# Keys and queries kept in memory with the head dimension first, keys padded to 384 columns: a two-layer cross-attention kernel on one Trainium2 core

## The reference

```python
q = hidden_state @ Wq + bq
k = encoder_hidden_state @ Wk + bk
v = encoder_hidden_state @ Wv + bv
q = q.reshape(b, l, KVH, GROUPS, HD).transpose(0, 2, 3, 1, 4)
k = k.reshape(b, s, KVH, HD).transpose(0, 2, 1, 3)
scores = jnp.einsum('bkgld,bksd->bkgls', q, k) * scale
scores = scores + encoder_attention_mask[:, :, None, :, :]
attn = jax.nn.softmax(scores, axis=-1)
out = jnp.einsum('bkgls,bksd->bkgld', attn, v)
x = out @ Wo + bo + hidden_state     # then a layer norm
```

## Time and profile before

| | us |
|---|---|
| median of 3 runs | 677.18 (675.15 to 677.86) |
| profiled execution, device time | 673.3 |
| its span, first to last instruction | 671.5 |
| PE busy | 646.0 (96%) |
| DVE busy | 497.7 (74%) |
| ACT busy, POOL busy | 394.8, 398.4 (59% each) |
| packets of the transfer queue, share of 16 engines | 66.9% |

### The profile page before, as it was taken

One profiled execution on the slowest core, in us unless ns is written; L12 is line 12 of the kernel. 1 busy time (PEld: TensorE's weight loads), 2 busy tenths in 40 slices (PEclk: granted clock), 3 DMA queues, 4 the chain that ended last, 5 costly groups with the idle time before them and its releaser, 6 DMA issues.

```text
span 671.5 us, 11880 instructions
## 1 busy us (share of the span) xinstructions
PE 646.0 (96%) x3737; PEld 470.4 (70%) x3737; DVE 497.7 (74%) x1455; ACT 394.8 (59%) x588; POOL 398.4 (59%) x255
## 2 busy tenths in 40 slices
PE   5998999999999999999999999999999999989987
PEld 2455666777777878777777768787777777756455
DVE  1547787887687787878787878878787888786742
ACT  3232675766657666656766676766567656656421
POOL 4328676775475766667665657676676667554220
PEclk9999898999999999999999999999999999999999
DMA  8898767576785776868584778666786857644212
GB/s 265 266 176 182 182 148 157 124 143 163 141 271 100 244 138 198 162 193 177 130 235 108 230 107 256 123 208 154 198 171 162 193 126 158 116 87 137 89 46 72
DMA packets 61072, 109.67 MB, mean 163 GB/s; under 512 B 11621, under 2 KB 49573, under 8 KB 60498
## 3 DMA queue, kind: packets, MB, share of 16 engines
q1 hardware_dynamic: 61010, 108.91, 66.9%
HBM read 86.37 MB, written 22.10 MB: 162 GB/s over the span
## 4 chain that ended last, share of the span: by engine, by line
PE 71%; DMA 9%; POOL 6%; issue 5%; DVE 3%; SPq 3%; ACT 1%; POOLq 0%; DVEq 0%; ACTq 0%
PE mx_ps L581 11%; PE work L540 10%; PE work L541 9%; PE work L542 9%; PE o_ps L597 7%; PE work L654 5%; PE work L705 5%; POOL pr L2490 4%; DMA late<-r_dr 4%; PE sc_ps L568 3%; PE sc_ps L569 3%; PE sc_ps L561 3%; PE work L610 2%; DMA k_dr<-k_l 1%; PE work L728 1%
## 5 line engine op out<-in xcount | busy, mean ns | idle before, releaser
L1549 DVE CUSTOM_DVE_ANT_0 mx_ps<-mx_ps,mask_n 100x361 f32<-100x361 f32 x512 | 270.9, 543 | 64.9 <-PE mx_ps L581 60.0
L2490 POOL TENSOR_TENSOR pr<-pr,mask_t 128x800 f32<-128x800 f32 x124 | 236.1, 1912 | 65.4 <-ACT pr L2056 65.2
L581 PE MATMUL mx_ps<-ks,qs 96*100 96x362 f32 x512 | 182.0, 372 | 3.9 <-DMA qs<-q_dr 1.9
L2063 ACT ACTIVATE pr<-pr 128x1200 f32<-128x1200 f32 x128 | 149.4, 1206 | 13.1 <-POOL pr L2490 6.1
L2056 ACT ACTIVATE pr<-sc_ps 128x800 f32<-128x800 f32 x124 | 104.0, 838 | 73.4 <-PE o_ps L597 47.2
L581 PEld LDWEIGHTS mx_ps<-ks,qs 96*100 96x100 f32 x512 | 84.7, 167 | 42.4 <-DVE mx L1549 11.9
L1535 DVE TENSOR_TENSOR pr<-sc_ps,mask_t 128x400 f32<-128x400 f32 x124 | 70.8, 571 | 24.1 <-PE sc_ps L561 15.3
L2502 POOL TENSOR_TENSOR c_l<-cT,c_h 128x1448 fp32r<-128x1448 f32 x16 | 55.0, 3439 | 52.5 <-ACT c_h L2090 52.5
L1549 DVE DVE_READ_ACCUMULATOR2_ANT mx<- 100x1 f32 x512 | 72.0, 141 | 0.0
L597 PE MATMUL o_ps<-pr,va 128*32 128x400 f32 (+1 forms) x768 | 71.2, 503 | 0.2 <-ACT pr L2063 0.2
L654 PEld LDWEIGHTS work<-late 128*128 128x128 f32 (+1 forms) x384 | 49.6, 191 | 6.9 <-issue 5.9
(11 more groups left out here) (167 smaller groups left out, 1232.4 us busy)
## 6 DMA issues: line engine op xcount, KB each, us to landing
qs<-q_dr SPq DMA_DIRECT2D x128, 100.0 KB, 4.3
late<-in_ctx SPq DMA_DIRECT2D x16, 768.0 KB, 6.6
cT<-in_ctxT SPq DMA_DIRECT2D x16, 724.0 KB, 4.9
ks<-k_dr SPq DMA_DIRECT2D x128, 90.5 KB, 4.0
late<-in_ctxT SPq DMA_DIRECT2D x16, 724.0 KB, 5.8
o_dr<-o_s SPq DMA_DIRECT2D x30, 200.0 KB, 3.3
xT<-in_xT SPq DMA_DIRECT2D x16, 200.0 KB, 4.2
q_dr<-q_h SPq DMA_DIRECT2D x16, 200.0 KB, 4.9
```

The lines of the kernel that those rows point to most:

```text
L581: nc.tensor.matmul(mx_ps[0:L, n % 2, 0:SP2], qs[p][0:TERMS, g, L * j:L * (j + 1)], ks[p][0:TERMS, g, 0:SP2], start=True, stop=True).then_i ...
L1549: V.tensor_tensor_reduce(out=src, in0=src, in1=mask_n[p][:, :], scale=1.0, scalar=-3.0e38, op0=ALU.add, op1=ALU.max, accum_out=mx[p][:, n: ...
L2063: A.activation(t, t, ACT.Exp).then_inc(ex_ok, 1)
L2490: G.tensor_tensor(t, t, mask_t[p][:, 1:3, :].unsqueeze(2).to_broadcast([P, 2, J, L]), ALU.add).then_inc(sc_pool, 1)
```

## The change

Keys and queries stand in device memory with the dimension first and the group second, and the keys are padded from 362 to 384 columns in `k_h` and `k_l` already. A row of one dimension over four groups is then one contiguous piece, in memory and in the stack: 4 x 384 x 4 = 6144 bytes of keys, 4 x 400 x 4 = 6400 of queries. A stack transfer of keys moves 16 pieces of 6144 bytes. The two query blocks of a call (high and low) are now one transfer over 32 partitions, since `q_dr` has its high and low part one behind the other. A half takes 6 transfers instead of 8. The stores must now scatter: each turns group first into dimension first, so the memory side has the shape 8 x 16 x columns. POOL clears the padding of `k_h` and `k_l` once at the start in place of the 22 columns of both `ks`. The waits count accordingly.

```diff
-        k_h, k_l = sb("k_h", [P, SP2], F32R), sb("k_l", [P, SP2], F32R)
+        k_h, k_l = sb("k_h", [P, SC * P], F32R), sb("k_l", [P, SC * P], F32R)
...
-        k_dr = nc.dram_tensor("k_dr", (2, 2, P, SP2), F32, kind="Internal").ap()
-        q_dr = nc.dram_tensor("q_dr", (2, 2, P, JL), F32, kind="Internal").ap()
+        k_dr = nc.dram_tensor("k_dr", (2, 2, HD, KVH, SC * P), F32, kind="Internal").ap()
+        q_dr = nc.dram_tensor("q_dr", (2, 2, HD, KVH, JL), F32, kind="Internal").ap()
...
                 for r in range(r0, r1):
-                    sp.dma_start(ks[p][HD * r:HD * (r + 1), gs, 0:SP2].bitcast(F32),
-                                 k_dr[p, r // 2, :, :].rearrange("(g d) s -> d g s", d=HD)[:, gs, :]
+                    sp.dma_start(ks[p][HD * r:HD * (r + 1), gs, :].bitcast(F32), k_dr[p, r // 2, :, gs, :]
                                  ).then_inc(st_in[half][p], 16)
-                    sp.dma_start(qs[p][HD * r:HD * (r + 1), gs, :].bitcast(F32),
-                                 q_dr[p, r % 2, :, :].rearrange("(g d) c -> d g c", d=HD)[:, gs, :]
-                                 ).then_inc(st_in[half][p], 16)
+                sp.dma_start(qs[p][HD * r0:HD * r1, gs, :].bitcast(F32),
+                             q_dr[p, :, :, gs, :].rearrange("r d g c -> (r d) g c")).then_inc(st_in[half][p], 16)
...
             def keys_out(b):
...
+                if b == 0:
+                    sp.wait_ge(zero_ok, 5)
-                wait(sp, st_in[0][p], 128 * (b // 2))
-                wait(sp, st_in[1][p], 128 * (b // 2))
-                sp.dma_start(k_dr[p, 0, :, :], k_h[:, :].bitcast(F32)).then_inc(k_out, 16)
-                sp.dma_start(k_dr[p, 1, :, :], k_l[:, :].bitcast(F32)).then_inc(k_out, 16)
+                wait(sp, st_in[0][p], 96 * (b // 2))
+                wait(sp, st_in[1][p], 96 * (b // 2))
+                sp.dma_start(k_dr[p, 0, :, :, :].rearrange("d g s -> g d s"), k_h[:, :].bitcast(F32)).then_inc(k_out, 16)
+                sp.dma_start(k_dr[p, 1, :, :, :].rearrange("d g s -> g d s"), k_l[:, :].bitcast(F32)).then_inc(k_out, 16)
...
+                pool.memset(k_h[:, SP2:SC * P].bitcast(F32), 0.0).then_inc(zero_ok, 1)
+                pool.wait_ge(zero_ok, 4)
+                pool.memset(k_l[:, SP2:SC * P].bitcast(F32), 0.0).then_inc(zero_ok, 1)
...
-                pool.memset(ks[p][0:64, :, SP2:SC * P].bitcast(F32), 0.0).then_inc(zero_ok, 1)
```

More of the change, by code:

```diff
@@ L323, in queries_out @@
                 wait(sp, ql_ok, b + 1)
-                wait(sp, st_in[0][p], 128 * (b // 2))
-                wait(sp, st_in[1][p], 128 * (b // 2))
-                sp.dma_start(q_dr[p, 0, :, :], q_h[:, :].bitcast(F32)).then_inc(q_out, 16)
-                sp.dma_start(q_dr[p, 1, :, :], q_l[:, :].bitcast(F32)).then_inc(q_out, 16)
+                wait(sp, st_in[0][p], 96 * (b // 2))
+                wait(sp, st_in[1][p], 96 * (b // 2))
+                sp.dma_start(q_dr[p, 0, :, :, :].rearrange("d g c -> g d c"), q_h[:, :].bitcast(F32)).then_inc(q_out, 16)
+                sp.dma_start(q_dr[p, 1, :, :, :].rearrange("d g c -> g d c"), q_l[:, :].bitcast(F32)).then_inc(q_out, 16)
             def keys_out(b):
@@ L554, in scores @@
                 if g == 0 and b < 2:
-                    pe.wait_ge(zero_ok, 8 + 5 * b)
+                    pe.wait_ge(zero_ok, 9 + 4 * b)
                 if b == 0 and g == 0:
@@ L574, in heads @@
                 if b < 2 and n0 == 0:
-                    pe.wait_ge(zero_ok, 6 + 5 * b)
+                    pe.wait_ge(zero_ok, 7 + 4 * b)
                 for n in range(n0, n1):
@@ L578, in heads @@
                     if n % (NH // 2) == 0:
-                        pe.wait_ge(st_in[n // (NH // 2)][p], 128 * (b // 2 + 1))
+                        pe.wait_ge(st_in[n // (NH // 2)][p], 96 * (b // 2 + 1))
                     wait(pe, a_mx, NH * b + n - 1)
@@ L1588, in k_low @@
                 wait(dve, k_out, 32 * b)
-                V.scalar_tensor_tensor(k_l[:, :], work[:, 1, 0:SP2], bk_c[:, 0:1], k_h[:, :].bitcast(F32),
+                V.scalar_tensor_tensor(k_l[:, 0:SP2], work[:, 1, 0:SP2], bk_c[:, 0:1], k_h[:, 0:SP2].bitcast(F32),
                                        ALU.add, ALU.subtract).then_inc(kl_ok, 1)
@@ L2151, in k_high @@
                 wait(act, k_out, 32 * b)
-                A.activation(k_h[:, :], work[:, 1, 0:SP2], ACT.Identity, bias=bk_c[:, 0:1]).then_inc(kh_ok, 1)
+                A.activation(k_h[:, 0:SP2], work[:, 1, 0:SP2], ACT.Identity, bias=bk_c[:, 0:1]).then_inc(kh_ok, 1)
             def v_cols(b):
@@ L2464, in constants, with one_rows @@
                 pool.wait_ge(zero_ok, 3)
+                pool.memset(k_h[:, SP2:SC * P].bitcast(F32), 0.0).then_inc(zero_ok, 1)
+                pool.wait_ge(zero_ok, 4)
+                pool.memset(k_l[:, SP2:SC * P].bitcast(F32), 0.0).then_inc(zero_ok, 1)
+                pool.wait_ge(zero_ok, 5)
             def zero_rows(p):
-                first = 3 + 5 * p
-                pool.memset(ks[p][0:64, :, SP2:SC * P].bitcast(F32), 0.0).then_inc(zero_ok, 1)
+                first = 5 + 4 * p
+                pool.memset(ks[p][64:TERMS, :, :].bitcast(F32), 0.0).then_inc(zero_ok, 1)
                 pool.wait_ge(zero_ok, first + 1)
-                pool.memset(ks[p][64:TERMS, :, :].bitcast(F32), 0.0).then_inc(zero_ok, 1)
+                pool.memset(qs[p][64:TERMS, :, :].bitcast(F32), 0.0).then_inc(zero_ok, 1)
                 pool.wait_ge(zero_ok, first + 2)
-                pool.memset(qs[p][64:TERMS, :, :].bitcast(F32), 0.0).then_inc(zero_ok, 1)
+            def one_rows(p):
+                first = 5 + 4 * p
+                pool.memset(ks[p][TERMS:ROWS, :, :].bitcast(F32), 1.0).then_inc(zero_ok, 1)
                 pool.wait_ge(zero_ok, first + 3)
[L2475 to L2478, removed]
                 if p == 1:
@@ L2481, in one_rows @@
                 pool.memset(va[p][:, :, :, HD:2 * HD], 1.0).then_inc(zero_ok, 1)
-                pool.wait_ge(zero_ok, first + 5)
+                pool.wait_ge(zero_ok, first + 4)
             def add_mask(b, g):
```

## The result

The changed kernel takes 670.65 us (median of 20 runs, 668.28 to 680.63), the kernel before 675.63 us in the same comparison (20 runs, 671.76 to 679.71): ratio 0.9942, interval 0.9921 to 0.9962. The ratio leaves out the changed kernel's two slow runs, 680.5 and 680.6 us (over 1.5% above its fastest), which its median includes; the medians lie 5.0 us apart. The three runs of before that the prediction started from stood 1.5 us above the median of the twenty.

The account below looks back on a forecast made before the run. PE, busy 96% of the span, was taken as the bound, with batches nearly late for their loads. Loop 0.75, start +0.6 - 0.3 and end -0.4 summed to +0.65 us: 677.8 us, 8-in-10 range 674.3 to 685.

Parts of the forecast that it names:

- Only waits can be won, the loop won't move: Whole kernel: only PE's waits for transfers, some 4 to 5 us, can be given back; a shorter path gives almost nothing.
- Stores cost 1.1 us each batch: Key stores in each batch: scattered to 8 groups, they run on half the engines and take 1.1 us more.
- Loads gain 0.75 us: Stack loads of a half: keys stay at 136 GB/s, queries on 32 partitions reach 200, 0.75 us less.
- X: Change in length of each batch's path from key store to last load: 1.1 - 0.75 = +0.35 us.
- Start: +0.6 - 0.3 us: Start: batch 1's key store adds 1.1, a saved issue takes 0.46; batch 0's head 16 gets about 0.3 back.
- End: -0.4 us: Head 16 of batch 15, waiting 1.29 us for loads: only the load gain counts, for half the loads, -0.4 us.
- The waits aren't there to be won: Argument against the rival of a faster kernel: PE hardly waits for transfers, so faster loads have little to win.
- The list of margins: Time to spare before the heads of batches 4 to 13, 0.0 to 1.4 us, 0.8 on average, from one profile.
- The base: Starting time: median of three runs, 677.18 us, 3.9 above the profiled 673.3; +0.65 us added, giving 677.8.
- Rival 2: Faster: loads gain over 1.1 us, X at -1 or below, waits go, about 3 us: 674.2 us; chance 0.13.
- Rival 1: Slower: stores on half the engines, no load gain, X = 1.3, PE waits, +6.4 us: 683.6 us; chance 0.29.

Follow-up runs that it names:

- half stores: Kernel before with only its key and query stores given 8 groups as outer count in memory, so on half the engines; loads unchanged: 683.51 us, ratio 1.0145.
- new order: Kernel before with only each call's loads reordered from keys, queries, keys, queries to keys, keys, queries, queries: 667.99 us, ratio 0.9892.
- start-only kernel: Kernel before with loads ordered keys, keys, queries, queries in batches 0 to 2 alone, the old order elsewhere: 670.96 us, ratio 0.9953.
- half stores with the old order: Two kernels loading keys, queries, keys, queries: kernel before with stores on half the engines, 1.0145; changed kernel with each query load split in two, 1.0124.
- blocks 32 apart: Kernel before loading keys, keys, queries, queries, first call taking blocks 0 and 2, second blocks 1 and 3: 684.29 us, ratio 1.0142.
- other order: Kernel before with each call's loads reordered: keys of block r, queries of r+1, queries of r, keys of r+1: 667.12 us, ratio 0.9876.
- the three kernels that lost: Kernel before with stores on half the engines, 1.0145; changed kernel with query loads split, old order, 1.0124; kernel before with neighbouring loads 32 partitions apart, 1.0142.
- full stores: Changed kernel with projection columns permuted to dimension first, so each store is 128 rows on all 16 engines: 666.4 us, ratio 0.9877.

## Why the prediction was wrong

Two steps failed: the order of the loads was priced at nothing, and the start was summed wait by wait, which gave it the wrong sign (+0.3 us, where the maxima came 2.35 us earlier).

- *Only waits can be won, the loop won't move:* right in the loop. It stayed at 36.8 to 36.9 us in the changed kernel, in spite of the faster loads.
- *Stores cost 1.1 us each batch:* right, 1.19 us. The Trainium skill's rule on the number of engines (page "DMA: Bandwidth & Descriptors", section "Why a DMA increments its semaphore by 16 and not by 1"), which the prediction cites, agrees with the half stores: share 0.47, 9 updates.
- *Loads gain 0.75 us:* mis-sized, 1.23 us. X was -0.04 us, not +0.35, so that the loop cost nothing, not 0.75 us. And the reason was wrong: the gain was put on the 32 partitions of the query load, 136 GB/s kept for the keys. It comes from the order of the loads, which the text ahead of the prediction saw in the issued rows ("with the keys of both blocks ahead of the queries") and which has no term in the sum: with the new order alone the loads of the kernel before take 7.9 us instead of 8.8.
- *Start: +0.6 - 0.3 us:* wrong in sign. Each wait was priced by itself. Between 30 and 57 us the DMA engines are full in the kernel before (share 1.03) while PE is busy for 26.4 of the 27 us, so PE doesn't show there what the loads of batch 0 gain. It passes on to everything behind them in the queue: the second half (landing 55.0 us instead of 57.1), the key store of batch 1 (60.2 instead of 60.9, though on half of the engines) and the maxima, which landed 2.60 us after their issue instead of 3.79. The start-only kernel shows it at 0.47%.
- *End: -0.4 us:* mis-sized. The changed kernel's lead grew by 1.4 us from the first heads of batch 15 to its head 16.
- *"The waits aren't there to be won":* wrong. The earlier trace rows and one wait of 0.5 us have 4.2 us of them, and 3.9 us were won, though not one for one. The terms as measured, nothing in the loop, 2.35 at the start and 1.4 at the end, sum to 3.8; that this comes so close is partly luck, since the two profiles differ in their falls of the clock and in the wait at 191.5 us.
- *The list of margins* came from one execution, which at 673.3 us was 2.3 us faster than the median of its kernel. With the half stores alone the loss was 9.8 us (1.45% of 675.5) where the same sum, at X = 1.1 and with 1.1 us at the start, gives 4.9. The clock can account for a part: its mean was 0.9888 against 0.9949, which is 2.5 us by the slope of time on clock over 66 runs of the kernel before, and 4.1 us at most (0.0061 of the time), both estimates. The rest is the margins that vary, or isn't known.
- *The base:* of the 7.2 us between 677.8 and 670.65, 1.5 us is that the three runs it started from stood high.
- *Rival 2*, with 0.13, was nearest in kind: the loads gained over 1.1 us and the waits went. But its condition, X at -1 or below, didn't come about, and its gain of 3 us was too small. It set the low end of the range.
- *Rival 1* did not come about in the changed kernel, but half stores with the old order gave 1.0145 and 1.0124, near its 683.6 us (683.5 and 683.1). That the first agrees so well is luck: its X was 1.1, not 1.3, and the base was another.

## What to carry to other kernels

Before a transfer is made longer or merged, look at which partitions it and its neighbours in the queue fill: in this kernel loads of 16 partitions did best when neighbours filled blocks whose partition numbers differ by 16, not by 0 or 32. A layout that wants scattered stores is better had by permuting the columns of the projection, so that the store stays 128 rows; here that only drew level with the new order of loads in the old layout. And a list of margins from one profile can understate what they cost: where most are below 1 us, take a second profile or widen the range on both sides. Price the start as a queue and not wait by wait.

## What the runs showed of the hardware

**Transfers of 16 partitions that collide.** With the same bytes, the same pieces and 16 partitions each, the DMA engines moved 130 GB/s (blocks 32 apart), 145 and 137 (the kernel before, two profiles), 159 (new order) and 164 (other order) from 1.5 to 5.5 us after the first load's issue, by order alone. The shares were 1.00, 0.95 and 0.99, 0.87 and 0.92: the slowest had the highest. A share near 1 thus doesn't say that the engines move what they can; the rate beside it tells more.

**The clock.** PE's granted clock falls to half, from 2.4 to 1.2 GHz, for stretches of 3.4 or 6.8 us. The places change from execution to execution, but not freely: in 8 of the 14 profiles one begins between 95 and 104 us, and in three at 195. In the kernel before (first) one began 1 us after PE's wait of 1.8 us for the maxima, in the changed kernel (second) 1.1 us after one of 2.1 us:

```profile
68.30:71.70 3.40, 3.40 (x9) 2.17 (x9) 2.29 (x9) 1.68 (x3) 1.88 (x1) 0.50 1.03 322
```

```profile
194.60:198.00 3.40, 3.40 (x25) 1.01 (x24) 0.59 (x3) 0.00 (x0) 0.00 (x0) 0.51 0.55 154
```

This is part of what spreads the times of one kernel: the changed kernel's runs at a mean clock of 1.000 took 668.3 to 668.7 us, those at 0.989 to 0.991 took 670.8 to 677.0. It explains little of the change. The mean over its runs, without the two of 680.5 us and more, is 0.9944; the clocks of the 20 runs it was compared with aren't on record, but 66 other runs of the kernel before have 0.9935 on average, and that difference would be 0.6 us at most. In the experiments the clock goes with the result: about 0.9885 in the three kernels that lost, with the most waits, and 0.9957 to 0.9975 in the new order, the other order and the full stores, against 0.9909 to 0.9949 in the kernel before. So a part of each ratio there is the clock's, whether as a consequence of the waits or by itself. And it makes a pair of profiles misleading, since the one of before has 10.2 us at half speed and the one of after 3.4.
